# Row maxima turned by VectorE in blocks, a weight slice moved up, and gathers issued ahead of pending sums

## What is computed

```python
# attention: 32 query heads of 16 features, 8 key heads; k = v = ctx
scores = einsum('bkgsd,bktd->bkgst', layernorm(x), ctx) / 4
x = x + tanh(g_xattn) * (softmax(scores) @ ctx)
# feed-forward: y = layernorm(x), 8192 tokens
probs = softmax(y @ Wr); topw, topi = top_k(probs, 4); topw /= sum(topw)
shared = (silu(y @ Wsg) * (y @ Wsu)) @ Wsd * sigmoid(y @ Wse)   # 1408 wide
# 32 experts, 352 wide; each takes its first 64 tokens at most
ye[e] = (silu(xe[e] @ Wg[e]) * (xe[e] @ Wu[e])) @ Wd[e]
x = x + tanh(g_ffn) * (shared + sum over the token's experts of w * ye)
```

## Time and profile before

| | |
|---|---|
| Time, median of 3 runs | 2355.34 us (2355.14 to 2355.68) |
| The profiled execution | 2355.15 us, of it the span 2353.3 us |
| PE busy | 2300.9 us (98%), 12545 instructions |
| DVE, ACT, POOL busy | 1137.8 (48%), 804.6 (34%), 585.7 us (25%) |
| Mean granted clock of TensorE | 0.993 |
| Chain that ended last | PE 66%, DVE 1%, DMA 1% of the span |
| DMA | 235.10 MB, mean 100 GB/s |

### The profile page before, as it was taken

One profiled execution on the slowest core, in us unless ns is written; L12 is line 12 of the kernel. 1 busy time (PEld: TensorE's weight loads), 2 busy tenths in 40 slices (PEclk: granted clock), 3 DMA queues, 4 the chain that ended last, 5 costly groups with the idle time before them and its releaser, 6 DMA issues.

```text
span 2353.3 us, 41796 instructions
## 1 busy us (share of the span) xinstructions
PE 2300.9 (98%) x12545; PEld 1775.7 (75%) x12545; DVE 1137.8 (48%) x2218; ACT 804.6 (34%) x1440; POOL 585.7 (25%) x1395
## 2 busy tenths in 40 slices
PE   7999999999998999999999999999999999999899
PEld 5777777777776877777777777778777787777577
DVE  6888888888886842232323323233222332223132
ACT  6888888888885111010110101011010110101010
POOL 5666666666663100000000000000000000000000
PEclk9999999999998999999999999999999999999899
DMA  3555455455545132222222222223222132223221
GB/s 81 137 145 140 133 142 141 138 136 142 143 131 169 19 116 79 85 96 80 84 78 72 106 80 85 78 64 115 78 87 78 62 115 79 87 78 116 85 72 43
DMA packets 271244, 235.10 MB, mean 100 GB/s; under 512 B 122337, under 2 KB 198113, under 8 KB 271202
## 3 DMA queue, kind: packets, MB, share of 16 engines
q1 hardware_dynamic: 266850, 221.90, 31.4%
q0 software_dynamic: 4352, 12.65, 1.7%
HBM read 161.88 MB, written 71.57 MB: 99 GB/s over the span
## 4 chain that ended last, share of the span: by engine, by line
PE 66%; DVE 1%; DMA 1%; issue 0%; DVEq 0%; POOL 0%; POOLq 0%
PE acc L1117 7%; PE p_u L1133 7%; PE p_u L1135 7%; PE p_u L1134 7%; PE acc L1118 7%; PE acc L1119 7%; PE p_g L1133 7%; PE p_g L1135 7%; PE p_g L1134 7%; PE p_x L1165 2%; PE p_y L1152 2%; PE p_x L1152 2%; PE p_x L1143 0%; DMA out_dram<-eo,cur_tok 0%; DMA rows<-out_dram 0%
## 5 line engine op out<-in xcount | busy, mean ns | idle before, releaser
L1051 DVE TENSOR_TENSOR act_f<-p_u,act_f 128x512 f32<-128x512 f32 x176 | 121.7, 691 | 998.1 <-PE p_u L1135 998.0
L956 ACT ACTIVATE act_f<-p_g 128x512 f32<-128x512 f32 x176 | 105.3, 598 | 1219.1 <-PE p_g L1135 1198.2
L559 DVE TENSOR_REDUCE negmax<-p_max 128x8 f32<-128x1024 f32 x256 | 313.2, 1223 | 80.9 <-PE p_max L701 67.3
L1117 PE MATMUL acc<-wd_h,hh 128*128 128x512 f32 x704 | 280.5, 398 | 0.0
L1133 PE MATMUL p_u<-xh,wgu_h 128*128 128x512 f32 x704 | 274.1, 389 | 4.0 <-DVE act_f L1051 4.0
L1133 PE MATMUL p_g<-xh,wgu_h 128*128 128x512 f32 x704 | 275.6, 391 | 0.0
L1118 PE MATMUL acc<-wd_l,hh 128*128 128x512 f32 x704 | 275.3, 391 | 0.0
L1119 PE MATMUL acc<-wd_h,hl 128*128 128x512 f32 x704 | 275.1, 391 | 0.0
L1135 PE MATMUL p_g<-xh,wgu_l 128*128 128x512 f32 x704 | 274.0, 389 | 0.0
L1135 PE MATMUL p_u<-xh,wgu_l 128*128 128x512 f32 x704 | 273.9, 389 | 0.0
L1134 PE MATMUL p_g<-xl,wgu_h 128*128 128x512 f32 x704 | 273.9, 389 | 0.0
(11 more groups left out here) (142 smaller groups left out, 3581.3 us busy)
## 6 DMA issues: line engine op xcount, KB each, us to landing
ew<-in_L_ffn_Wg_dram SPq DMA_DIRECT2D x32, 704.0 KB, 6.0
ew<-in_L_ffn_Wu_dram SPq DMA_DIRECT2D x32, 704.0 KB, 7.3
xs<-in_x_dram SPq DMA_DIRECT2D x64, 256.0 KB, 2.7
xres<-in_x_dram SPq DMA_DIRECT2D x64, 256.0 KB, 2.8
out_dram<-x SPq DMA_DIRECT2D x64, 256.0 KB, 2.0
xn_rows<-xn SPq DMA_DIRECT2D x64, 256.0 KB, 3.0
xn_cols<-xnT SPq DMA_DIRECT2D x64, 256.0 KB, 2.5
rows<-out_dram SPq DMA_DIRECT2D x16, 1024.0 KB, 5.3
```

The costliest lines, as they stand in the source:

```text
L559: nc.vector.tensor_reduce(negmax[c % 2][:, :].rearrange("p (g i) -> p i g", i=G), p_max[:, :, :].rearrange("p a (h g t) -> p (a h) g t", g ...
L1117: mm(acc[:, j, :], a[:, t], wd_h[:, f, :], start=(f == 0), stop=False)
```

## The change

Five edits.

1. The maxima. The reductions of two chunks write into one [128, 32] tile (columns: group, chunk, head), `negmax[c // 2]`. After chunks 1 and 3 DVE waits for its own reduction and turns the tile with `nc.vector.transpose`, 32 by 32 in each block of 32 partitions, to `maxT`. SP sends it in four transfers, one per block (16 partitions of 32 numbers each to 8 places of 32 numbers in partitions 0 and 64 of `qt`): at chunk 0 those of (B-1; 2, 3), at chunk 2 those of (B; 0, 1). PE waits at chunks 0 and 2 alone. PE's transpose, ACT's copy and `p_mt` are gone.
2. POOL's weight slice stands before its routing work instead of after.
3. `gather_x(p + 1)` is issued within `expert(p)`, after the first gather of `eo` and before the wait for the sum. It waits for PE's transposes of the old `xe` (`xeT_mm`) and DVE's use of its weights (`cur_w_set`).
4. For that `y1` leaves `xe`: it shares a buffer with `eh` and `ehT`, and ACT waits for the pair's last sum (`eo_done`) before it writes `eh`.
5. DVE waits for the expert numbers (`eof_set`) after the first split and `route_start` instead of before.

```diff
-            negmax = [sb(f"negmax{i}", [128, 8]) for i in range(2)]
-            mt = [sb(f"mt{i}", [8, 128], F32R) for i in range(2)]
+            negmax = [sb(f"negmax{i}", [128, 32]) for i in range(2)]
+            maxT = [sb(f"maxT{i}", [128, 32]) for i in range(2)]
...
+            MROW = 16 * 4
...
                     for c in range(NC):
-                        m = (B - 1, 3) if c == 0 else (B, c - 1)
-                        if m[0].ok:
-
-                            b, cc = m
-                            wait(sp, mt_done, 4 * b.n + cc + 1)
-                            for g2 in range(2):
-                                sp.dma_start(qt[b.par][64 * g2:64 * g2 + 1, cc, :].bitcast(F32),
-                                             mt[cc % 2][4 * g2:4 * g2 + 4, :].bitcast(F32)).then_inc(mrow_in[cc % 2], 16)
+                        b, h = (B - 1, 1) if c == 0 else (B, 0)
+                        if c % 2 == 0 and b.ok:
+
+                            wait(sp, maxT_done, 2 * b.n + h + 1)
+                            row = qt[b.par][0:65:64, 2 * h:2 * h + 2, :].bitcast(F32).rearrange("p c (i s) -> p (c i) s", i=G)
+                            for q in range(4):
+                                sp.dma_start(row[:, :, 32 * q:32 * q + 32], maxT[h][32 * q:32 * q + 16, :]).then_inc(mrow_in[h], 16)
...
+                    if weights_split(B):
+                        pool.wait_ge(whi_done, B.pair + 1)
+                        alone(pool, spare_p)
+                        nc.gpsimd.tensor_tensor(w_cols(wgu_l, B.pair), wst_cols, w_cols(wgu_h, B.pair).bitcast(F32), ALU.subtract).then_inc(wlo_done, 1)
                     b = B - 4
...
-                    if weights_split(B):
-                        pool.wait_ge(whi_done, B.pair + 1)
...
-                            act.wait_ge(mt_mm, 4 * b.n + cc + 1)
-                            wait(act, mrow_in[cc % 2], 32 * (2 * b.n + cc // 2))
-                            nc.scalar.activation(mt[cc % 2][:, :], p_mt[:, :], ACT.Copy).then_inc(mt_done, 1)
...
-                            wait(dve, mt_mm, 4 * B.n + c - 1)
-                            nc.vector.tensor_reduce(negmax[c % 2][:, :].rearrange("p (g i) -> p i g", i=G),
+                            if c % 2 == 0:
+                                wait(dve, maxT_done, 2 * (B.n - 1) + c // 2 + 1)
+                            nc.vector.tensor_reduce(negmax[c // 2][:, 0:16].rearrange("p (g c i) -> p c i g", g=2, c=2)[:, c % 2, :, :].bitcast(F32R),
                                                     p_max[:, :, :].rearrange("p a (h g t) -> p (a h) g t", g=2, t=128),
                                                     AX.X, ALU.max, negate=True).then_inc(max_done, 1)
+                            if c % 2 == 1:
+
+                                dve.wait_ge(max_done, 4 * B.n + c + 1)
+                                wait(dve, mrow_in[c // 2], MROW * B.n)
+                                nc.vector.transpose(maxT[c // 2][:, :], negmax[c // 2][:, :]).then_inc(maxT_done, 1)
...
-                            pe.wait_ge(mrow_in[c % 2], 32 * (2 * b.n + c // 2 + 1))
+                            if c % 2 == 0:
+                                pe.wait_ge(mrow_in[c // 2], MROW * (b.n + 1))
...
-                            pe.wait_ge(max_done, 4 * b.n + cc + 1)
-                            wait(pe, mt_done, 4 * b.n + cc)
-                            last = tr(p_mt[:, :], negmax[cc % 2][:, :], ident[:, :])
-                            last.then_inc(mt_mm, 1)
...
-            eh = sb("eh", [128, FE])
-            ehT = sb("ehT", [128, 3, 128])
+            ebuf = sb("ebuf", [128, FE + 3 * 128])
+            eh = ebuf[:, 0:FE]
+            ehT = ebuf[:, FE:FE + 3 * 128].rearrange("p (c t) -> p c t", c=3)
+            y1 = ebuf[0:CAP, 0:E]
...
-            y1 = xe[0:CAP, 0:E]
...
-                def expert(p, rows_before):
-
+                def gather_x(p):
                     wait(pool, xeT_mm, p)
-                    wait(pool, eo_done, 2 * p)
+                    wait(pool, cur_w_set, p)
                     alone(pool, spare_p2)
-                    nc.gpsimd.tensor_copy(cur_idx[:, :], slot_idx[:, bass.ts(p, 1)])
+                    nc.gpsimd.tensor_copy(cur_idx[:, :], slot_idx[:, bass.ts(p, 1)]).then_inc(idx_set, 1)
+                    pool.wait_ge(idx_set, p + 1)
+                    alone(pool, spare_p2)
+                    nc.gpsimd.indirect_dma_start(out=xe[:, :], out_offset=None, in_=xn_dram,
+                                                 in_offset=bass.IndirectOffsetOnAxis(ap=cur_idx[:, 0:1], axis=0)).then_inc(xe_in, 16)
+
+                def expert(p, rows_before, more):
...
                     for h in range(2):
                         nc.gpsimd.indirect_dma_start(out=eo[:, :], out_offset=None, in_=out_rows,
...
+                        if h == 0 and more:
+                            gather_x(p + 1)
...
                                 act.wait_ge(eg_mm, e.p + 1)
+                                wait(act, eo_done, 2 * e.p)
...
-                dve.wait_ge(eof_set, 2)
-
                 def body(i, pairs):
                     if is_first(i):
                         split_x(0, x_first)
                         route_start()
+                        dve.wait_ge(eof_set, 2)
```

More of the change, by code:

```diff
@@ L181, in build @@
             p_ot = ps("p_ot", [128, 512])
-            p_mt = ps("p_mt", [8, 128])
             x_in = [sem(f"x_in{i}") for i in range(2)]
@@ L202, in build @@
             tq_mm, k_mm, p1_mm, p2_mm = sem("tq_mm"), sem("k_mm"), sem("p1_mm"), sem("p2_mm")
-            pv_mm, ot_mm, mt_mm = sem("pv_mm"), sem("ot_mm"), sem("mt_mm")
+            pv_mm, ot_mm = sem("pv_mm"), sem("ot_mm")
             xnT_mm, lg_mm = sem("xnT_mm"), sem("lg_mm")
             max_done, exp_done, tq_done = sem("max_done"), sem("exp_done"), sem("tq_done")
-            kt_done, pv_done, mt_done = sem("kt_done"), sem("pv_done"), sem("mt_done")
+            kt_done, pv_done, maxT_done = sem("kt_done"), sem("pv_done"), sem("maxT_done")
             ot_done, x2_done, xnT_done, lg_done = sem("ot_done"), sem("x2_done"), sem("xnT_done"), sem("lg_done")
             FIRST, LAST = 5, 61
+            MROW = 16 * 4
             def iterations(eng, body, count=None):
@@ L396, in body @@
                                                 key_of[:, bass.ts(b.n, 1)].to_broadcast([128, NE]), ALU.mult)
-                    if weights_split(B):
-                        pool.wait_ge(whi_done, B.pair + 1)
-                        alone(pool, spare_p)
-                        nc.gpsimd.tensor_tensor(w_cols(wgu_l, B.pair), wst_cols, w_cols(wgu_h, B.pair).bitcast(F32), ALU.subtract).then_inc(wlo_done, 1)
                 chain.per_turn = 2 * (1 + 1 + 1 + 1 + 1)
@@ L455, in body @@
                             q_evac(B + 1, 0)
-                        b, cc = (B - 1, 3) if c == 0 else (B, c - 1)
-                        if b.ok:
-                            act.wait_ge(mt_mm, 4 * b.n + cc + 1)
-                            wait(act, mrow_in[cc % 2], 32 * (2 * b.n + cc // 2))
-                            nc.scalar.activation(mt[cc % 2][:, :], p_mt[:, :], ACT.Copy).then_inc(mt_done, 1)
                     if weights_split(B):
@@ L477, in _ @@
                 nc.vector.memset(kt[1][:, :, :].bitcast(F32), 0.0).then_inc(pads, 1)
+                nc.vector.memset(negmax[0][:, :], 0.0)
+                nc.vector.memset(negmax[1][:, :], 0.0)
                 nc.vector.memset(ks[:, :, 0:16], 0.0).then_inc(dve_chain, 1)
@@ L787, in build @@
             spare_p2, spare_s2 = sem("spare_p2"), sem("spare_s2")
+            idx_set = sem("idx_set")
             cur_set, wcur_set, eo_zero = sem("cur_set"), sem("wcur_set"), sem("eo_zero")
@@ L907, in expert @@
                     pool.wait_ge(cur_set, p + 1)
-                    alone(pool, spare_p2)
-                    nc.gpsimd.indirect_dma_start(out=xe[:, :], out_offset=None, in_=xn_dram,
-                                                 in_offset=bass.IndirectOffsetOnAxis(ap=cur_idx[:, 0:1], axis=0)).then_inc(xe_in, 16)
                     pool.wait_ge(rows_out, 16 * rows_before)
@@ L925, in expert @@
                         alone(pool, spare_p2)
-                expert(0, 1)
+                gather_x(0)
+                expert(0, 1, True)
                 with pool.Fori(1, NT - 2) as p:
-                    expert(p, p + 1)
-                expert(NT - 2, NT - 2)
-                expert(NT - 1, NT - 1)
+                    expert(p, p + 1, True)
+                expert(NT - 2, NT - 2, True)
+                expert(NT - 1, NT - 1, False)
             @block.scalar
```

## The result

| | before | after |
|---|---|---|
| median of the runs | 2355.44 us | 2386.76 us |
| profiled execution, its span | 2355.15, 2353.3 us | 2388.18, 2386.1 us |
| first stage, to the first feed-forward product | 751.2 us | 798.9 us |
| second stage, from there to the end | 1602.1 us | 1587.3 us |
| period of chunk 3's reduction, mean of some 50 turns | 11.13 us | 11.87 us |

The ratio is 1.0135, with an interval of 1.0121 to 1.0148: 1.35% slower, 28.5 us over the predicted 2358.3 and just inside the range (2342 to 2388), by luck, as will be seen: the range reached so far only for the sake of rival C. The second stage gained 14.8 us; the first lost 47.6.

The account below looks back on a forecast made before the run. It took PE to lead the first stage, with a wait for POOL's query stacks, and to fill the second but for one gap. 2355.15 - 14.1 (gathers) + 16.2 (longer turns) + 1 (run-out) = 2358.3 us, range 2342 to 2388.

Parts of the forecast that it names:

- rival C: SP's new-form transfers issue more slowly; at +0.12 us each the turn is 11.9 us, time 2388; chance 0.17.
- Gathers ahead: -14.1: Second stage, tile 14: PE's 11.25 us gap goes, and 2.9 us more from the full clock behind it.
- VectorE's turning: 0.37 us each: First stage, DVE: two turnings a turn, each waiting for its own reduction, each add 0.37 us to the queue.
- Transfers: 2.55 to issue, 1.14 to land: First stage, SP: a burst of four transfers takes 2.55 us to issue, and the last lands 1.14 us later.
- The slice: query stacks 0.95 us earlier, and the 0.52 between the turns goes: First stage, POOL: the slice runs in 2.58 us of idleness, so query stacks come 0.95 us earlier and turns equalise.
- Three loops, and the slowest counts: 11.4 us a turn: First stage: the slowest of three loops sets the turn at 11.4 us, +16.2 us in some 60 turns.
- loop (c): First stage, through SP's queue: chunk 0's transfers wait behind six others; 22.8 us for two turns, 11.4 each.
- A: First stage: SP's queue sets the turn, 11.25 to 11.6 us, time 2349 to 2370; chance 0.46.
- B: First stage: the chain keeps up and DVE sets the turn at 11.18 us or less, 2345 at 11.18; chance 0.31 together.
- D: Second stage: a new condition of the gather comes late and tile 14's gap stays, time 2372; chance 0.06.
- The sign that I named last: First stage: the prediction is wrong if PE's short idle times, once a turn, bring its clock down; no size given.

Follow-up runs that it names:

- in halves: The kernel before with POOL's weight slice moved ahead of the routing flags, and that slice cut into two instructions of half the columns: 2362.6 us, ratio 1.0029.
- the flags ahead: The kernel after, with VectorE's cast of the indices and its flags of the chosen experts placed ahead of chunk 3's reduction: 2352.05 us, ratio 0.999.
- the rows ahead of the keys: The kernel after, with SP's four transfers for chunks 0 and 1 issued before the load of the keys: 2363.35 us, ratio 1.0036.
- the weight loads: The kernel after with VectorE's flags and chunks 0 and 1's transfers ahead, plus both weight loads issued behind chunks 2 and 3's transfers: 2341.01 us, ratio 0.9938.
- as idle ones: The kernel before with gathers and VectorE's flags moved ahead, plus two turnings of an unused tile a turn on VectorE: 2361.12 us, ratio 1.0021.
- the version with flags and rows ahead: The kernel after, with VectorE's flags ahead of chunk 3's reduction and chunks 0 and 1's transfers ahead of the load of the keys: 2361.6 us, ratio 1.0028.

## Why the prediction was off, step by step

The direction was right and the range held, but by luck: the loop that set the turn is in none of the terms, and the miss of 28.5 us is nearly as large as the 31.3 measured.

**Gathers ahead: -14.1.** Right, in size and in its two parts. Alone it measured -13.6, and in the kernel after the second stage is 14.8 us shorter: PE's transposes of the fifteenth pair stand 11.6 us earlier in the stage (2225.99 - 798.87 beside 2189.99 - 751.23), and the rest came behind them, where the clock stayed at the 2.4 GHz level.

**VectorE's turning: 0.37 us each.** Right. The duration was 0.21. The next instruction started 0.44 us later than it would have after chunk 1 (409.82, where 409.47 - 0.09 is the usual start) and 0.34 after chunk 3 (403.52 beside 403.18): 0.78 a turn where I had 0.74. The Trainium skill ("VectorE: DVE Perf Modes", the DRAIN that can't be avoided), by which the wait on itself costs nothing extra, would have made it 0.26 in all. After chunk 3 the turning started 0.03 us behind the listed end of the reduction and after chunk 1 0.13 behind, both later than the overlap of 0.09 that an instruction without such a wait has. The page measured copies in a row; for this pair of instructions the measurement goes against it.

**Transfers: 2.55 to issue, 1.14 to land.** Too dear: a burst of four takes 2.17 us to issue. From the end of the turning (403.51) to the end of the issue (405.71) are 2.2 us. The landing was right: 1.09 us from the end of the issue (413.55) to PE's scores (414.64). Rival C named the right time, 2388, by a mechanism that did not happen.

**The slice: query stacks 0.95 us earlier, and the 0.52 between the turns goes.** This is the step that failed. I costed the slice's new place by POOL's queue alone: it fitted into an idle time of 2.58 us, so I booked it as free. It isn't, because the instruction that ends this idle time is on DVE, and DVE's normalising and cast are held up while the slice runs. Alone it cost 7.2 us where my step said about -16. The Trainium skill has this rule ("SBUF — State Buffer", "Who interferes with whom"): VectorE and GpSimd share one pair of ports of the on-chip memory as an exclusive lock, and the one that issues second "fully blocks"; on VectorE's side it holds only for instructions that use the shared pair, not for all. The rows agree in the order: 1.14 instead of 0.54 us beside a slice that ended at 406.47, and in halves the stall was handed on in the order of issue. The stall is somewhat shorter than a full block would make it (0.60 us where 0.86 of the slice were left).

**Three loops, and the slowest counts: 11.4 us a turn.** The term of the sum that was off. It measured 11.87, and 0.47 us in 60 turns is 28.2 of the 28.5 us missed. The list lacked a fourth loop, POOL's, which was in the trace: I had read that the longer turn holds the wait for POOL, but struck this loop out with the slice. In fact the change lengthened it at each of its stations: the turning went in between the reduction and is_top (+0.34 on DVE), the slice held up the cast (+0.51), POOL's addition was held up by a normalising (+0.31), and the slice no longer covered the branch (+0.41). Against these stands the slice's own place in the loop, about 1 us. From chunk 3's reduction to the end of the query stacks it was 10.10 us before (400.00 to 410.10) and is 10.56 now (402.04 to 412.60), and by these 0.46 the turn went from 11.39 to 11.85. In my loop (c) the leg of 2.78 us for the loads and stores of chunk 1's place was taken from a turn in which POOL's key stacks were early. After the change it is, counted the same way, 4.47 us (406.90 to 411.37), with 1.77 us of SP standing still before the load of the keys. The two edits that undo these, the flags ahead and the rows ahead of the keys, took 35 and 23 us off the kernel after, each alone, and 46 together once the weight loads made room.

**A, B, C, D.** None of the four rivals had POOL in it. A came nearest in that PE did wait for the rows, 0.78 us as I had said, though only in every second turn; but what made them late was a wait inside the queue, and not its length. B's bound by VectorE (11.13 to 11.18) is real, but only once POOL's loop and the holds in SP's queue are gone: 11.25 with the flags ahead, 11.07 with the queue in order too.

The sign that I named last, PE's short idle times bringing its clock down, did not come: the granted clock from 60 to 710 us is 1.00 in the kernel after.

**What stays open.** Why, with the flags ahead, the slice costs more behind them than in front of them (12 and 23 us), while in the kernel before, with the flags late, its place behind them is the cheaper one by 7 us. A part is the clock in the run-out; the rest is not settled. DVE's instructions that meet POOL change their lengths with every shift between the two, and no run held that shift fixed. And between the first and the fifth turn the kernel after loses 4.1 us, more than 0.74 a turn; no run looked into that.

## What to carry to other kernels

Idle time of one engine is only free for work that does not stop the engine it is waiting for: before filling a gap, look at which engine ends it, and whether that engine's instructions lengthen when the two run together. When a wait is to be removed, go once around the whole loop it belongs to and list every queue in it, with the waits inside the queue, for two turns; a loop that is "struck out" by one edit must be summed again with all the other edits in it. And an engine with one idle moment of 0.4 us a turn can't take two instructions of 0.2 us that wait for their predecessors: here they came to 0.78 us a turn, or 0.55 as idle ones, and with what they shifted on to POOL's instructions to 32 us in the end.

## What the runs showed of the hardware

- Some pairs of a tile operation on POOL and one on DVE took turns. The one behind is stretched by most of what is left of the first: DVE's normalising from 0.54 to 1.14 us (0.60, where 0.86 were left), a cast of four columns from 0.16 to 0.67 (0.51 of 0.64), is_top from 0.28 to 0.65 (0.37 of 0.51). The first keeps its length. It goes both ways: an addition on POOL that started 0.09 us behind a normalising took 0.56 instead of 0.25 us. Other pairs don't meet: the reductions that read the scores' banks kept their 1.21 to 1.23 us in every version, and the statistics, which read on-chip memory, took 0.70 us beside POOL's query stacks (410.87 in the kernel after) as elsewhere.
- Four transfers of 16 pieces of 128 bytes on a side take 2.17 us to issue, 0.54 each, while two of the old ones, in pieces of 512, take 1.24, 0.62 each.
- TensorE's mean granted clock can differ from execution to execution of one kernel, and the time with it: the version with flags and rows ahead took 2356.5 us at a mean granted clock of 0.997 and 2366.6 at 0.991.
- The order of a handful of instructions on POOL and SP, none of them longer than a microsecond and the set always the same, moved this kernel by 44 us (2341 to 2385, five orders with the flags ahead).
